# One PSUM bank for the attention outputs of a pair of sequences: two heads per group of 32 partitions

## What is computed

```python
x = x + _L0_xattn_ref(_layernorm(x, axis=-1), ctx_2048, ...)   # banded, local_size 64, then relu * ctx, @ w_ct
x = x + _L0_ffn_ref(_layernorm(x, axis=-1), ...)
x = x + _L1_xattn_ref(_layernorm(x, axis=-1), ctx_2048, ...)   # k, v from ctx; rotary
x = x + _L1_ffn_ref(_layernorm(x, axis=-1), ...)
...
scores = jnp.einsum('bqhd,bkhd->bhqk', q, k) / jnp.sqrt(jnp.asarray(d, q.dtype))   # H = 8 heads, d = 8
attn = jax.nn.softmax(scores, axis=-1)
o = jnp.einsum('bhqk,bkhd->bqhd', attn, v).reshape(n, t, e)
o = o @ w_out.T + b_out
```

## Time and profile before

| | us |
|---|---|
| median of 3 runs | 1414.41 |
| lowest and highest run | 1407.34, 1414.45 |
| the profiled execution, its own time | 1412.66 |
| its span in the trace | 1410.9 |
| PE busy | 1291.8 |
| DVE busy | 952.0 |
| ACT busy | 874.6 |
| POOL busy | 712.6 |

### The profile page before, as it was taken

The page is one execution under the profiler, slowest core; times in us unless marked ns, Lnnn a source line. Parts: engine busy times, 40 slices in busy tenths (PEclk is TensorE's granted clock), DMA queues, the critical chain, the costliest instruction groups (busy, mean ns, idle before and its releaser), DMA issues.

```text
span 1410.9 us, 37590 instructions
## 1 busy us (share of the span) xinstructions
PE 1291.8 (92%) x11228; PEld 889.4 (63%) x11228; DVE 952.0 (67%) x2163; ACT 874.6 (62%) x1910; POOL 712.6 (51%) x1297
## 2 busy tenths in 40 slices
PE   4888999999999988773799999999999989999998
PEld 2566777777777765562466666666666655766675
DVE  5866878888778887368788888888888862111110
ACT  2555666766666666462688888888888874122211
POOL 4466777777777786305456556556556511010000
PEclk8899999999999999895799999999999999999999
DMA  8455444444444441003344444444444310000000
GB/s 200 107 147 138 96 94 104 98 91 95 98 102 92 94 96 39 12 0 72 70 103 103 98 102 104 96 101 106 94 100 109 88 40 1 16 30 15 15 15 30
DMA packets 90803, 113.32 MB, mean 80 GB/s; under 512 B 13779, under 2 KB 82131, under 8 KB 83059
## 3 DMA queue, kind: packets, MB, share of 16 engines
q1 hardware_dynamic: 86912, 107.05, 33.2%
q10 hardware_dynamic: 3830, 5.49, 1.3%
HBM read 18.66 MB, written 4.19 MB: 16 GB/s over the span
## 4 chain that ended last, share of the span: by engine, by line
PE 60%; POOL 12%; issue 11%; DVE 8%; DMA 3%; ACT 2%; POOLq 1%; SPq 1%; DVEq 1%; ACTq 0%
PE bank L468 10%; PE bank L429 9%; PE bank L656 8%; PE bank L647 8%; PE bank L445 8%; PE bank L427 5%; PE bank L479 4%; DVE row_max L1044 3%; PE bank L510 3%; POOL rot L1232 2%; PE bank L618 2%; POOL Qp L1221 2%; PE bank L499 1%; POOL k_rest L1237 1%; POOL q_rest L1237 1%
## 5 line engine op out<-in xcount | busy, mean ns | idle before, releaser
L1044 DVE TENSOR_REDUCE row_max<-bank 128x2 f32<-128x384 f32 (+1 forms) x1024 | 599.7, 617 | 131.0 <-PE bank L429 128.9
L692 ACT ACTIVATE probs<-bank 128x384 f32<-128x384 f32 (+1 forms) x1024 | 534.3, 542 | 174.0 <-PE bank L445 167.4
L445 PE MATMUL bank<-Qs,Ks 128*128 128x192 bf16 (+1 forms) x2048 | 369.4, 262 | 23.6 <-ACT probs L692 16.3
L429 PE MATMUL bank<-Ks,Qs 96*128 96x192 bf16 (+1 forms) x2048 | 373.9, 265 | 13.3 <-DMA Ks<-Ks 8.5
L1250 POOL TENSOR_SCALAR_AFFINE_SELECT probs<-probs 128x256 f32<-128x256 f32 (+1 forms) x512 | 260.8, 533 | 147.2 <-ACT probs L692 128.5
L429 PEld LDWEIGHTS bank<-Ks,Qs 96*128 96x128 bf16 x2048 | 190.2, 99 | 124.2 <-issue 40.3
L468 PE MATMUL bank<-probs,V 128*32 128x192 f32 (+1 forms) x4096 | 251.6, 364 | 5.9 <-POOL probs L1250 4.6
L445 PEld LDWEIGHTS bank<-Qs,Ks 128*128 128x128 bf16 x2048 | 190.0, 98 | 51.1 <-ACT probs L692 27.8
L427 PE MATMUL bank<-band,ident 128*128 128x384 bf16 x512 | 170.6, 333 | 8.5 <-DMA Ks<-Ks 7.5
L468 PEld LDWEIGHTS bank<-probs,V 128*32 128x32 f32 x4096 | 108.5, 110 | 86.3 <-issue 46.0
L1187 DVE TENSOR_TENSOR X<-bank,X 128x256 f32 (+1 forms) x32 | 13.6, 424 | 185.6 <-PE bank L656 185.6
(11 more groups left out here) (125 smaller groups left out, 1704.1 us busy)
## 6 DMA issues: line engine op xcount, KB each, us to landing
Ks<-Ks SPq DMA_DIRECT2D x64, 576.0 KB
Qs<-Qs SPq DMA_DIRECT2D x128, 192.0 KB
Qs<-Qp SPq DMA_DIRECT2D x192, 64.0 KB
Ks<-Kp SPq DMA_DIRECT2D x192, 64.0 KB
side<-in_ctx SPq DMA_DIRECT2D x64, 128.0 KB, 2.0
X<-in_x SPq DMA_DIRECT2D x4, 1024.0 KB, 13.9
out<-X SPq DMA_DIRECT2D x8, 512.0 KB, 2.9
Qs<-max_rows SPq DMA_DIRECT2D x128, 12.0 KB
```

The costliest lines, as they stand in the source:

```text
L429: last = nc.tensor.matmul(dst[:, blk * win:(blk + 1) * win], Qs[0:SHIFT_ROW, pair[1], h, blk * P:(blk + 1) * P], Ks[0:SHIFT_ROW, pair[1], ...
L445: last = nc.tensor.matmul(dst[:, blk * win:(blk + 1) * win], Ks[:, pair[1], h, blk * P:(blk + 1) * P], Qs[:, pair[1], h, start(blk):start( ...
L692: nc.scalar.activation(probs[:, h % 8, 0:2 * win], exp_bank[h % 2][:, 0:2 * win], ACT.Exp, scale=SCALE).then_inc(s["exped"], 1)
L1044: nc.vector.tensor_reduce(row_max[:, pair[1], h, :], bank_of(pair, h)[:, 0:2 * win].rearrange("p (b k) -> p b k", b=2), AX.X, ALU.max).the ...
```

## The change

Heads of an even and of the following odd group share 32 partitions of the output: the even group's head writes rows 0 to 8 of them, the odd group's head rows 9 to 17. This is done in the weights: `V` has 9 columns of zeros between the groups' blocks (`V_STEP` = 137 words per block of four heads), and for an odd group the 32 columns are read from 9 columns further left, so that values and ones land 9 rows lower and zeros come before them. The odd group accumulates onto the even group. So group 0 and 1 together fill one half of `pv_bank`, group 2 and 3 the other, and a pair's outputs fit the bank once. The middle `heads_out`, `turn_heads` and `normalise` of each pair are gone, with the job `heads0` in the cycle of bank A; the late ones are as large as before for copy and transposes, and `normalise` handles 32 denominators and 256 values per partition where it handled 16 and 128. Group 2 no longer waits for a copy. The order of the normalised channels changes, for which rows of `w_out` and entries of the bias of V are permuted on the host (not shown). Nothing else moves.

```diff
+V_STEP = 4 * 32 + HD + 1
...
 JOBS = {
-    "A": [("q", AHEAD), ("heads1", -1), ("v", 2), ("max0", 1), ("heads0", 0)],
+    "A": [("q", AHEAD), ("heads", -1), ("v", 2), ("max0", 1)],
     "B": [("max1", 0), ("k", AHEAD), ("back", -1), ("out", -1), ("mix", -1)],
...
-        V = sb("V", [P, RING, 2, HPP, 32])
+        V = sb("V", [P, RING, 2 * 4 * V_STEP])
...
-        heads_sb = sb("heads_sb", [P, 2, 2 * T])
-        rcp = sb("rcp", [P, 2, HPP])
-        normed = sb("normed", [P, RING, 2, P])
+        heads_sb = sb("heads_sb", [P, 2 * T])
+        rcp = sb("rcp", [P, HPP, 2])
+        normed = sb("normed", [P, RING, 2, 2, CH])
...
-                if g % 2 == 0:
-                    wait_some(e, s["heads_out"], num(pair) * 2 + g // 2)
+                if g == 0:
+                    wait_some(e, s["heads_out"], num(pair))
                 dst = pv_bank
                 for blk in range(2):
                     for j in range(4):
                         head = 4 * g + j
-                        first = (g % 2) * T + start(blk)
+                        first = (g // 2) * T + start(blk)
+                        column = (blk * 4 + g) * V_STEP + 32 * j - (g % 2) * (HD + 1)
                         last = nc.tensor.matmul(dst[32 * j:32 * j + 32, first:first + win],
-                                                V[:, pair[1], blk, head, :],
+                                                V[:, pair[1], column:column + 32],
                                                 probs[:, head % 8, blk * win:(blk + 1) * win],
-                                                start=(blk == 0), stop=(blk == 1), skip_group_check=True)
+                                                start=(g % 2 == 0 and blk == 0), stop=(g % 2 == 1 and blk == 1),
+                                                skip_group_check=True)
                 last.then_inc(s["pv_done"], 1)
...
-            def turn_heads(pair, half):
-
-                if not active(pair):
-                    return
-                wait_bank(e, s, l, "A", f"heads{half}", pair)
-                e.wait_ge(s["heads_out"], num(pair) * 2 + half + 1)
+            def turn_heads(pair):
+
+                if not active(pair):
+                    return
+                wait_bank(e, s, l, "A", "heads", pair)
+                e.wait_ge(s["heads_out"], num(pair) + 1)
                 for blk in range(2):
-                    for g in range(2):
-                        last = nc.tensor.transpose(job_bank["A"][:, (blk * 2 + g) * P:(blk * 2 + g + 1) * P],
-                                                   heads_sb[:, half, g * T + blk * P:g * T + (blk + 1) * P],
+                    for seq in range(2):
+                        last = nc.tensor.transpose(job_bank["A"][:, (2 * blk + seq) * P:(2 * blk + seq + 1) * P],
+                                                   heads_sb[:, seq * T + blk * P:seq * T + (blk + 1) * P],
                                                    ident[:, :])
                 last.then_inc(s["A_filled"], 1)
...
-                    if h == 14:
-                        turn_heads(r, 0)
                     score_head(p1, h)
                     shifted_head(r, h)
...
-                nc.scalar.activation(V[:, pair[1], :, :, 0:HD].rearrange("p b h d -> p (b h) d"),
-                                     job_bank["A"][:, 0:2 * P].rearrange("p (n d) -> p n d", d=HD),
+                wide = V[:, pair[1], :].rearrange("p (n c) -> p n c", c=V_STEP)[:, :, 0:4 * 32]
+                nc.scalar.activation(wide.rearrange("p n (j c) -> p n j c", c=32)[:, :, :, 0:HD],
+                                     job_bank["A"][:, 0:2 * P].rearrange("p (n j d) -> p n j d", j=4, d=HD),
                                      ACT.Copy).then_inc(s["A_read"], 1)
...
-            def heads_out(pair, half):
-                if not active(pair):
-                    return
-                e.wait_ge(s["pv_done"], num(pair) * 4 + 2 * half + 2)
-                wait_job(e, s, l, "A", f"heads{half}", at(pair, -1), "filled")
-                nc.scalar.activation(heads_sb[:, half, :], pv_bank[:, :],
+            def heads_out(pair):
+                if not active(pair):
+                    return
+                e.wait_ge(s["pv_done"], num(pair) * 4 + 4)
+                wait_job(e, s, l, "A", "heads", at(pair, -1), "filled")
+                nc.scalar.activation(heads_sb[:, :], pv_bank[:, :],
                                      ACT.Copy).then_inc(s["heads_out"], 1)
...
-                        heads_out(m1, 1)
+                        heads_out(m1)
...
-                    if h == VALUES_AT[l] + 9:
-                        heads_out(r, 0)
                     exp_head(r, h)
...
-            def normalise(pair, half):
-
-                if not active(pair):
-                    return
-                wait_job(e, s, l, "A", f"heads{half}", pair, "filled")
-                turned = job_bank["A"][:, :].rearrange("p (n c) -> p n c", c=32)
-                nc.vector.reciprocal(rcp[:, half, :], turned[:, :, HD]).then_inc(s["rcp_done"], 1)
-                e.wait_ge(s["rcp_done"], num(pair) * 2 + half + 1)
+            def normalise(pair):
+
+                if not active(pair):
+                    return
+                wait_job(e, s, l, "A", "heads", pair, "filled")
+                turned = (job_bank["A"][:, :].rearrange("p (n c) -> p n c", c=32)[:, :, 0:2 * (HD + 1)]
+                          .rearrange("p n (i d) -> p n i d", i=2))
+                nc.vector.reciprocal(rcp[:, :, :], turned[:, :, :, HD]).then_inc(s["rcp_done"], 1)
+                e.wait_ge(s["rcp_done"], num(pair) + 1)
                 wait_job(e, s, l, "B", "back", at(pair, -RING), "filled")
                 nc.vector.tensor_tensor(
-                    normed[:, pair[1], :, half * CH:(half + 1) * CH].rearrange("p b (h d) -> p b h d", d=HD),
-                    turned[:, :, 0:HD].rearrange("p (b h) d -> p b h d", b=2),
-                    rcp[:, half, :].rearrange("p (b h) -> p b h", b=2).unsqueeze(3)
-                    .broadcast_to([P, 2, HEADS, HD]),
+                    normed[:, pair[1], :, :, :].rearrange("p a b (j i d) -> p (a b j) i d", i=2, d=HD),
+                    turned[:, :, :, 0:HD], rcp[:, :, :].unsqueeze(3).broadcast_to([P, HPP, 2, HD]),
                     ALU.mult).then_inc(s["A_read"], 1)
...
-                        normalise(m1, 1)
+                        normalise(m1)
...
-                    if h == 14:
-                        normalise(r, 0)
                     maximum(p1, h)
...
-            nc.gpsimd.memset(V[:, :, :, :, :], 0.0).then_inc(cleared_q, 1)
+            nc.gpsimd.memset(V[:, :, :], 0.0).then_inc(cleared_q, 1)
             e.wait_ge(cleared_q, 2)
-            nc.gpsimd.memset(V[:, :, :, :, HD:HD + 1], 1.0).then_inc(cleared_q, 1)
+            ones = V[:, :, :].rearrange("p a (n c) -> p (a n) c", c=V_STEP)[:, :, 0:4 * 32]
+            nc.gpsimd.memset(ones.rearrange("p n (j c) -> p n j c", c=32)[:, :, :, HD:HD + 1], 1.0).then_inc(cleared_q, 1)
```

23 lines of the change are left out of this document (12 added, 11 removed).

## The result

The changed kernel takes 1387.91 us (median of four runs, 1386.80 to 1393.43), the kernel before beside it 1414.0 us (1407.34 to 1414.45). The ratio is 0.9834, with a 95% interval of 0.9801 to 0.9868. The forecast was 1386 us in a range of 1376 to 1402. So the time came out as forecast. The sum behind it did not: one stage was right to a hundredth of a microsecond, another gave a third of what was booked for each of its pairs, and the start of the kernel made up most of the difference.

The account below looks back on a forecast made before the run. PE was taken to bound the kernel. Savings of 20.0 (steady pairs) + 1.7 (end of first attention) + 5.7 (other pairs) + 0 = 27.4 us gave 1385.3 or 1387.0, forecast 1386 us, range 1376 to 1402.

Parts of the forecast that it names:

- What PE gives back per transpose: At h=14, four removed transposes free 0.435 us of PE per pair, 20.0 us over 46 steady pairs.
- The first wait at L499/L502 stays 0.40 us: First attention, transpose of row maxima: PE's wait for max_parts stays 0.40 us, so a pair gains 0.44, not 0.57.
- the 0.07 us margin: First attention: only 0.07 us separate PE's and DVE's pacing of head 0's maximum; rival that DVE paces, 1383 us, chance 0.08.
- The second attention: Steady pairs there fall by the full 0.435 us, to 14.79 us; nothing booked for ScalarE's lost copy.
- The longer normalisation reaches POOL: Second attention, h=5: rival that larger normed delays k's rotation and POOL, up to 5 us back, 1391 us, chance 0.11.
- All groups in one bank: Products with V: rule implies a 0.6 us copy per pair, 38 us; booked 0, given 1.52 us of room.
- The loads of V: Weight loads at odd starts stay 110 ns, booked 0; rival that they slow, up to 127 us, 1512, chance 0.04.
- The masks: First attention, h=15: rival that group 2's product waits for POOL's mask, losing up to 12 us, likely 1391, chance 0.08.
- The end of the first attention: Three pairs where PE waits at L499 for DVE, which also dequantises weights: 0.57 us each, 1.7 us gain.
- The start: Near the start, two pairs waiting for the DMA of max_rows give 0; other pairs there give 0.435 us each.

Follow-up runs that it names:

- the two moves: Changed kernel with transposed row maxima one head later: first attention's second half, h=3 to h=4, 1386.12 us; second attention's first half, h=12 to h=13, 1387.67 us.

## Why the prediction was right, and where it was not

- **What PE gives back per transpose** (0.435 us for four, not the records' 1.09). Right. The steady first attention gave 15.89 - 15.45 = 0.44 us a pair. By the record of 272 ns the gain would have been 70 us; the whole change gave 23 to 26. The Trainium skill, "TensorE: Matmul & The Clock Gate", Part 4: PE-mode transpose, gives about 275 ns in the context of a kernel; the page measured bf16, and this trace has 273 ns for the record of an fp32 transpose.
- **The first wait at L499/L502 stays 0.40 us, since PE's scores of head 0 pace it.** Right, by the period of 15.45 us, by DVE's work put back without effect there, and by its disappearance when the transpose moved one head on. From the start of head 0's scores to this transpose it takes 2.35 us in the kernel before (317.46 to 319.81), in the changed one (318.83 to 321.18) and with DVE's work put back (308.49 to 310.84). DVE's timeline shows the 0.07 us margin held: the run of three maxima starts at 318.07 and its third, 0.56 us before the run's end at 319.75, starts at 319.19, right after head 0's scores end at 318.83 + 0.33 = 319.16.

```profile
318.07 1.68 DVE L1044 TENSOR_REDUCE row_max<-bank 128x2 f32<-128x384 f32 x3
319.68 0.57 DVE L945 TENSOR_SCALAR max_parts<-row_max 128x16 bf16<-128x16 f32 x1
...
318.83 0.33 PE L430 MATMUL bank<-Ks,Qs 96*128 96x192 bf16 x2
```

- **The second attention.** Wrong, in the step "ScalarE is not what L499 waits for in the stretch that loses it, so I book nothing", and already in "No idle time stands before them, so in a row of work without gaps it is given back in full". That PE does not idle before an instruction does not say that it won't idle behind it once the instruction is gone. The trace of before showed it, in rows that I did not read against each other:

```profile
895.45 0.38 PE L445 MATMUL bank<-Qs,Ks 128*128 128x256 bf16 x2
...
896.77 0.38 PE L445 MATMUL bank<-Qs,Ks 128*128 128x256 bf16 x2
...
895.87 1.08 ACT L692 ACTIVATE probs<-bank 128x512 f32<-128x512 f32 x2 [0.19 <-PE bank L445]
```

Head 14's shifted scores stood at 896.77. Without the transposes they would stand at 896.77 - 0.435 = 896.33. But head 12's exponential starts at 895.87, takes 0.54 us, and PE follows 0.09 us behind its end in the rows of after: 896.50. The transposes filled 0.17 us by this estimate, 0.19 by the trace of after. That term was 0.435 and should have been 0.25; the 0.09 us at h=5 and at L502 make the 0.15 us that came. In the first attention a head is 0.50 us of PE's work, two are 1.00, and the projection of the mix stands before head 14 besides, which is why the same removal was given back in full there.
- **The longer normalisation reaches POOL.** Booked at 0, with up to 0.19 us as a rival. The product takes 0.42 us (0.29 before), the wait at L502 grew by 0.03 us. The rotation on DVE is over at 867.73 + 0.47 = 868.20 and POOL's own half at 868.26, so the room held, if only just:

```profile
867.53 0.73 POOL L1229 TENSOR_TENSOR rot<-rot,rope 128x256 f32<-128x256 f32 x1 [1.59 <-ACT rot L722]
...
867.73 0.47 DVE L1064 SCALAR_TENSOR_TENSOR rot<-bank,att_b,rope 128x256 f32<-128x256 f32 x1
```

- **All groups in one bank** (the rule on rotating banks of the Trainium skill, "Perfetto Trace Analysis", Matmuls, from which the prediction estimated a loss of 38 us). No such loss at pv_bank: with the transposes back the kernel equals the one before within 0.2%. A wait for a bank to be emptied came elsewhere, at the two banks of the exponentials, though they do rotate.
- **The loads of V.** Booked at 0, right: 110 ns, and a group of the first attention still spans 0.79 us (317.87 to 318.66).
- **The masks.** The waits of L468/L470 for them do not appear in either steady stretch. Right.
- **The end of the first attention**, 3 x 0.57 = 1.7 us. Wrong: nothing came. DVE's work there did become shorter, but PE still waits for it, 6.9 us against 5.8 of before in three pairs:

```profile
PE bank L502 <- DVE max_parts L951: 6.9, 3, 2.8
```

Some steps of the dequantisation on DVE last longer than before; that they collide with POOL's masks was only thought of and not tried. The clock does not explain it away: the last pair but one takes 17.11 and 17.12 us in the two profiles, one of each kernel, in which it is 1.00 there, and 18.24 and 18.32 us in two where it is 0.91. No gain in either.
- **The start**, 2.2 us booked, about 6 found. Missed on the other side: the two transfers' pairs were booked at nothing and the rest at PE's own 0.435 us, though the first four pairs take 17 to 23 us there and depend on DMAs that compete with the weights. And PE's work was priced at a granted clock of 1.00, which does not hold there: the fall to 0.50 behind a wait, and its absence in the changed kernel's profile, make some 4 us of the profiled difference.

So 27.4 us were forecast and 23 to 26 came: 7.6 us too much for the second attention and 2 for the end of the first, against some 4 to 7 too little at the start. That the total came within 2 us of the forecast is luck: two terms were too large by 9.6 us together, one too small by 4 to 7. The chance of 0.11 for "normalisation delays POOL", at 1391, names the right stage and the wrong wait.

## What to carry to other kernels

An instruction on the bound engine that stands without idle time before it may still be covering a latency behind it: when it goes, look for the next use of each double buffer that follows, and compare the round trip through the other engine (here 1.07 us) with the work that is left between (0.88 us). A wait that a removal leaves in place can often be moved away by one step, but list first who has the same bank behind it and which DMA starts from it; here the two moves gave 0.12 and 0.13 us where waits of 0.40 and 0.52 stood, and a third, which took the bank's next user one step on, made the first of them 0.56. Price a wait by the distance of starts against a step without one: the 0.40 us in the list stood for 0.56.

## What was not expected of the hardware

- Four transposes of 128x128 fp32 have records of 273 ns and take PE 0.435 us together, 0.11 us each; put back alone, they cost 24 us in 64 pairs, or 0.37 us a pair.
- Loading 32 columns of fp32 weights takes 110 ns on the mean, whether all of the loads start at multiples of 32 words of `V` or one in twelve.
- 4 MB of weight loads issued in the first pairs lengthen the first seven by some 9 us. With them go PE's waits for a DMA of 12 KB and part of the time at the lower clock.
- A wait of 3.7 us was followed by a granted clock of 0.50 for the next 4.9 us at least, in which PE did 31 matmuls instead of 52. The length of the wait alone does not decide this: in another execution it stayed at 1.00 behind 3.1 us and fell behind 2.1 us.
